# A small load issued earlier, and eight TensorE warm-up matmuls in place of fourteen, at the start of a three-block attention kernel

## The chip, the cores and the metric

The kernel runs on one core of one Trainium2 chip. The metric is device time in microseconds (us) of one execution. The profile adds one profiled execution of the same program. TensorE is called PE in the profile, its weight load PEld, VectorE DVE, ScalarE ACT, GpSimd POOL, and SyncE SP.

## What is computed

Two sequences (b = 0 and 1) of 128 rows by 512 columns go through three residual blocks: a cross-attention block, an RWKV-7 block of which every row is its own short sequence, and an attention block with experts. Only the first block's start is touched by the change:

```python
# x: (2, 128, 512)
h = _layernorm(x, axis=-1)                 # no gain, no bias
Q, K, V = h @ Wq1, h @ Wk1, h @ Wv1
energy = einsum('bqd,bkd->bqk', Q, K)      # causal, masked beyond a counted length
z = softmax(energy / sqrt(32)) @ V
x1 = layer_norm(h + z, ln1_g, ln1_b)
z = cross_attn(x1, ctx_1024, Wq2, Wk2, Wv2)   # 2048 context rows a sequence
...
# RWKV block: x + (xprev - x) * mu_k, mu_a, mu_r, mu_w, mu_v, mu_g, six matmuls
```

The tensor `cols` holds the six mu vectors and the bias of the cross-attention block's first feed-forward layer, turned into 28 columns of 128 numbers.

## The kernel before

Everything is written out by hand, one block of code for each engine, with semaphores between them. An engine works through its list in order, so a wait holds up all that stands behind it. `s_x[b]`, `s_cols` and the `s_place[...]` semaphores count DMA landings; the others (`normed`, `turned`, `prod`, `evict` and so on) count finished steps of an engine, and the index 0 or 1 is the sequence.

**SyncE** issues all loads in one list. `fetch(name)` loads one block of 1 MB (a weight, or 512 context rows) into one of twelve places of `ring`; where the place was used before, it first waits for the block there to be done with. The list begins: X[0], k1, X[1], q1, ct01, `colv`, v1, ct02, ct00, two rows of gains, k2, q2 and on. The reads of `cols` go to `colv` (line 345).

**VectorE** begins with `start(0)`, the statistics of X[0] (lines 858, 860, 862); then, after GpSimd's power for the deviation (line 1786), `norm(0, "x")` (line 866), which gives Y[0]. Then it waits for `s_cols`, computes `rest` = 1 - mu from `colv` (line 1232), and goes on with `start(1)`, `k1_out(0)` (line 905), `norm(1, "x")` (line 866 again), `low("ct01")` (line 888) and `energies(0)`. `rest` itself is first used in the second block, over 100 us later.

**TensorE** begins with 14 matmuls of a matrix of ones into a bank that nobody reads. Then it turns Y[0] with four transposes (`in_halves`, line 416), multiplies by the weights k1 and q1 (`k1(0)`, `q1(0)`, line 442), turns Y[1] (`turned_rows(1, ...)`, line 405), and computes the energies `e1(0)` (line 401, 128x128), the values `v1(0)` (line 401, 128x512), a count, and `k1(1)`. One fp32 matmul stands in the trace as two records (passes). `mm` is the helper of line 401.

**ScalarE** copies the turned halves of Y[0] (`copy_halves`), splits ct01 (`split`, a copy of 128x2048), and evicts the two halves of q1 (`out_halves`), in this order. All its copies have line 1485. `e1(0)` waits for the eviction of q1.

**GpSimd** first makes constants: `ones`, the counters, `ident`, `mhalf`.

Of the kernel before, what the change touches and what calls it, by code (L numbers as in the profile page):

```python
# [76 lines left out]
def build(nc, blocks, xin, vecs, cols, out):  # L77
    with ExitStack() as ctx:
        def sb(name, shape, dt=F32):
            return ctx.enter_context(nc.sbuf_tensor(name, shape, dt))  # L80

        def sem(name):
            return ctx.enter_context(nc.semaphore(name))
# [13 lines left out]
        colv = sb("colv", [128, 28])  # L97
# [133 lines left out]
        s_cols, s_bc0, s_bc1, s_bc2 = (sem(n) for n in ("s_cols", "s_bc0", "s_bc1", "s_bc2"))  # L231
# [80 lines left out]
        def used(name):  # L312

            if name.startswith("ct"):
                return score[int(name[2])].at(name[3])
            if name[0] == "c":
                return gath[int(name[1])].at(name[2])
            return prod[1].at({"rk": "k", "ra": "a", "rw": "w", "rr": "r", "rv": "v", "rg": "g"}.get(name, name))
# [5 lines left out]
        @block_.sync  # L324
        def _(eng):
            s = Waits(eng)

            def fetch(name, first=False):
                before = [m for m in BLOCKS if PLACE[m] == PLACE[name] and NTH[m] == NTH[name] - 1]
                for m in before:  # L330
                    s.wait_ge(*used(m))
                    if m[0] != "c":
                        s.wait_ge(*prod[0].at({"rk": "k"}.get(m, m)))
                eng.dma_start(ring[:, PLACE[name], :], blocks[BLOCKS.index(name), :, :]).then_inc(  # L334
                    s_place[PLACE[name]], 16)

            def spread(first, end):
                return vecs[first:end, :].unsqueeze(0).broadcast_to([128, end - first, 512])

            eng.dma_start(X[0], xin[0, :, :]).then_inc(s_x[0], 16)  # L340
            fetch("k1")
            eng.dma_start(X[1], xin[1, :, :]).then_inc(s_x[1], 16)
            fetch("q1")
            fetch("ct01")
            eng.dma_start(colv[:, :], cols).then_inc(s_cols, 16)
            fetch("v1")
            fetch("ct02")
            fetch("ct00")
            eng.dma_start(bc[:, 0:2, :], spread(0, 2)).then_inc(s_bc0, 16)
            fetch("k2")  # L350
            fetch("q2")
            fetch("ct11")
            eng.dma_start(bc[:, 2:FIRST_BC, :], spread(2, FIRST_BC)).then_inc(s_bc1, 16)
            fetch("ct12")
            fetch("ct10")
            fetch("ct03")
            fetch("c03")
            fetch("ct13")
            fetch("c00")
            fetch("c01")  # L360
            fetch("c02")
            fetch("c10")
            fetch("f1")
            fetch("v2")
            fetch("c13")
            fetch("c11")
            fetch("c12")
            fetch("f2")
            fetch("ro")
            s.wait_ge(*used("c13"))  # L370
            fetch("rw")
            fetch("rk")
            fetch("rv")
            s.wait_ge(*used("c12"))
            fetch("fg")
            fetch("ra")
            s.wait_ge(*used("c11"))
            fetch("rf")
            fetch("fq")
            s.wait_ge(*normed[0].at("n4"))  # L380
            s.wait_ge(*normed[1].at("n4"))
            eng.dma_start(bc[:, 0:len(BCAST) - FIRST_BC, :], spread(FIRST_BC, len(BCAST))).then_inc(s_bc2, 16)
            fetch("rr")
            fetch("fk")
            fetch("fo")
            fetch("rg")
            s.wait_ge(*out_v[0].at("fin"))
            eng.dma_start(out[0, :, :], X[0]).then_inc(s_y[0], 16)
            s.wait_ge(*out_v[1].at("fin"))
            eng.dma_start(out[1, :, :], X[1]).then_inc(s_y[1], 16)  # L390
            s.wait_ge(s_y[0], 16)
            s.wait_ge(s_y[1], 16)
# [4 lines left out]
        def _(eng):  # L397
            s = Waits(eng)

            def mm(o_, l, r, first, last):  # L400
                return t.matmul(o_, l, r, start=first, stop=last)  # L401
# [293 lines left out]
                    i.then_inc(*fo_t[b].inc("fo"))  # L695

            s.wait_ge(*const.at("ones"))
            for _ in range(14):
                mm(psum[:, 7, 0:128], ones[:, :], ones[:, :], True, True)
            s.wait_ge(*const.at("ident"))  # L700
            s.wait_ge(*normed[0].at("x"))
# [1269 lines left out]
```

## Time and profile before

| | us |
|---|---|
| three runs | 237.29, 235.38, 237.14 |
| median | 237.14 |
| profiled execution, its own time | 237.29 |
| its span, first to last instruction | 235.6 |
| PE busy | 226.2 (96%) |
| DVE busy | 162.6 (69%) |
| ACT busy | 92.4 (39%) |
| POOL busy | 77.4 (33%) |

The own time of the profiled execution is 1.7 us over its span; this remainder lies around the first and the last instruction. "Busy" counts an engine's compute instructions, not its waits. Times in a row of the trace are counted from the start of the span. The share `PEclk` is the clock that TensorE was granted: 1.00 is 2.4 GHz, 0.50 is 1.2 GHz. It is a record of changes, so ahead of the first change it shows 1.00 whatever the clock was; there the length of a matmul's record tells it.

### The profile page before, as it was taken

The page shows a single profiled execution, that of the slowest core. Times are in us where ns is not written, and L with a number is a line of the kernel's source. Part 1 is how long each engine was busy: PE and PEld are TensorE (multiplying, and loading weights), DVE is VectorE, ACT ScalarE, POOL GpSimd, SP SyncE. Part 2 cuts the span into 40 slices and gives each one's busy share as a digit, 9 for nine tenths or more (in the row PEclk, how much of TensorE's full clock was granted, in tenths as well). Part 3 has the DMA queues.
Part 4 walks back from the last instruction along what each step waited for, and adds up shares of the span by engine and source line. Part 5 has one row for each costly group of instructions (what it writes and reads, how often), then busy time and mean ns, then how long its engine had stood idle before and what let it go on. Part 6 is the DMA issues. An engine that isn't in the chain of part 4 may idle for free.

```text
span 235.6 us, 3079 instructions
## 1 busy us (share of the span) xinstructions
PE 226.2 (96%) x1148; PEld 160.5 (68%) x1148; DVE 162.6 (69%) x310; ACT 92.4 (39%) x190; POOL 77.4 (33%) x78
## 2 busy tenths in 40 slices
PE   8989999999999999999999999999999699999994
PEld 8976969789888788587384444444444279799951
DVE  2084464696889985970566275699988879798961
ACT  2141415283469668704034244675421201251300
POOL 5040005038426415960051027635223118160000
PEclk9999999999999999999999999999999979999999
DMA  6999899505695599008996499000000000000011
GB/s 242 421 422 395 316 449 388 225 1 179 236 430 224 191 420 426 36 3 314 431 427 252 126 372 424 18 0 0 0 0 4 0 0 0 3 0 1 3 45 45
DMA packets 6351, 43.99 MB, mean 187 GB/s; under 512 B 832, under 2 KB 832, under 8 KB 1472
## 3 DMA queue, kind: packets, MB, share of 16 engines
q1 hardware_dynamic: 6336, 43.80, 46.3%
q8 instruction: 9, 0.15, 0.2%
q14 instruction: 6, 0.05, 0.1%
HBM read 43.27 MB, written 0.52 MB: 186 GB/s over the span
## 4 chain that ended last, share of the span: by engine, by line
PE 86%; DVE 5%; DMA 4%; ACT 2%; SPq 1%; issue 1%; POOL 0%; DVEq 0%
PE psum L401 68%; PE psum L442 13%; DMA colv<-cols 4%; PE psum L405 3%; ACT slots L1485 2%; PE psum L416 1%; DVE small L858 1%; DVE slots L866 1%; PE psum L547 1%; DVE slots L870 1%; SPq L334 1%; POOL small L1786 0%; DVE small L860 0%; DVE psum L1004 0%; DVE slots L882 0%
## 5 line engine op out<-in xcount | busy, mean ns | idle before, releaser
L401 PE MATMUL psum<-ring,slots 128*128 128x512 f32 (+3 forms) x228 | 92.5, 554 | 1.4 <-ACT slots L1485 1.3
L401 PEld LDWEIGHTS psum<-ring,slots 128*128 128x128 f32 (+1 forms) x228 | 40.4, 194 | 42.9 <-issue 37.6
L1485 ACT ACTIVATE slots<-psum 128x256 f32<-128x256 f32 (+4 forms) x58 | 24.4, 447 | 84.7 <-PE psum L401 37.9
L401 PE MATMUL psum<-ring_r,slots_r 128*128 128x512 f32 x192 | 46.2, 396 | 0.0
L1791 POOL TENSOR_TENSOR ring_r<-ring,ring_r 128x640 fp32r<-128x640 f32 x16 | 32.2, 2026 | 30.0 <-ACT ring_r L1485 30.0
L401 PEld LDWEIGHTS psum<-ring_r,slots_r 128*128 128x128 f32 x192 | 35.5, 188 | 9.0 <-ACT slots_r L1485 1.0
L442 PE MATMUL psum<-slots,ring 128*128 128x128 f32 x320 | 37.6, 277 | 0.5 <-ACT slots L1485 0.5
L442 PEld LDWEIGHTS psum<-slots,ring 128*128 128x128 f32 x320 | 36.5, 192 | 1.1 <-ACT slots L1485 1.0
L1485 ACT ACTIVATE ring_r<-ring 128x2048 fp32r<-128x2048 f32 x16 | 30.4, 1913 | 13.0 <-DMA ring<-blocks 7.6
L1786 POOL TENSOR_TENSOR small<-small,mhalf 128x1 f32<-128x1 f32 x16 | 8.8, 552 | 68.7 <-DVE small L862 68.7
L888 DVE TENSOR_TENSOR ring_r<-ring,ring_r 128x1408 fp32r<-128x1408 f32 x16 | 27.5, 1724 | 4.0 <-ACT ring_r L1485 4.0
L1795 POOL TENSOR_TENSOR slots<-slots,bc 128x512 f32<-128x512 f32 x9 | 11.9, 1326 | 15.3 <-DMA bc<-vecs 7.5
L401 PEld LDWEIGHTS psum<-slots,ring 128*128 128x128 f32 x128 | 14.6, 192 | 0.4
L401 PE MATMUL psum<-slots,ring 128*128 128x128 f32 x128 | 14.9, 276 | 0.0
L1485 ACT ACTIVATE slots<-psum,small 128x128 f32<-128x128 f32 (+1 forms) x20 | 8.8, 532 | 6.0 <-PE psum L405 3.3
L416 PEld LDWEIGHTS psum<-ident,slots 128*128 128x128 f32 x44 | 5.0, 141 | 6.9 <-DVE slots L876 2.6
L405 PE MATMUL psum<-ident,slots 128*128 128x128 f32 x60 | 8.3, 276 | 1.3 <-DVE slots L866 1.0
L1485 ACT ACTIVATE slots_r<-psum 128x512 fp32r<-128x512 f32 (+1 forms) x11 | 5.9, 564 | 9.2 <-PE psum L442 5.0
L401 PE MATMUL psum<-slots 64*128 64x128 f32 (+2 forms) x68 | 9.1, 300 | 0.0
L405 PEld LDWEIGHTS psum<-ident,slots 128*128 128x128 f32 x60 | 6.8, 140 | 3.3 <-DVE slots L866 1.2
L1795 POOL TENSOR_TENSOR slots<-slots 128x512 f32<-128x512 f32 x6 | 7.6, 1272 | 3.6 <-ACT slots L1485 2.8
L416 PE MATMUL psum<-ident,slots 128*128 128x128 f32 x44 | 6.9, 279 | 1.9 <-DVE slots L866 1.8
(170 smaller groups left out, 232.8 us busy)
## 6 DMA issues: line engine op xcount, KB each, us to landing
ring<-blocks SPq DMA_DIRECT2D x36, 1024.0 KB, 9.5
bc<-vecs SPq DMA_DIRECT2D x1, 3072.0 KB, 13.3
bc<-vecs SPq DMA_DIRECT2D x1, 1280.0 KB, 6.8
slots<-xin SPq DMA_DIRECT2D x2, 256.0 KB, 3.9
bc<-vecs SPq DMA_DIRECT2D x1, 512.0 KB, 17.4
y<-slots SPq DMA_DIRECT2D x2, 256.0 KB, 2.0
colv<-cols SPq DMA_DIRECT2D x1, 14.0 KB, 9.2
```

The lines of the kernel that those rows point to most:

```text
L334: eng.dma_start(ring[:, PLACE[name], :], blocks[BLOCKS.index(name), :, :]).then_inc(s_place[PLACE[name]], 16)
L401: return t.matmul(o_, l, r, start=first, stop=last)
L405: i = t.transpose(o_[:, c * 128:(c + 1) * 128], x[:, c * 128:(c + 1) * 128], ident[:, :])
L416: i = t.transpose(psum[:, bk1 if c > 1 else bk0, c * 128:(c + 1) * 128], src[:, c * 128:(c + 1) * 128], ident[:, :])
L442: i = t.matmul(psum[:, bk, e * 128:(e + 1) * 128], w[:, c, e * 128:(e + 1) * 128], srcw[:, c, b * 128:(b + 1) * 128], start=c == 0 and (e ...
L547: i = t.matmul(bank(4 * b + n), pick_r[:, n, :], pen_r[b], start=False, stop=True, skip_group_check=True)
L858: v.bn_stats(st[b], x).then_inc(*own_v.inc())
L888: v.tensor_tensor(ring_r[:, p, 0:CUT], ring[:, p, 0:CUT], ring_r[:, high(name), 0:CUT], ALU.subtract).then_inc(*split_low.inc(name))
L1485: return a.activation(o, x, func, **kw)
L1786: g.tensor_tensor(rs[b], ve[b], mhalf[:, 0:1], ALU.pow).then_inc(*rstd[b].inc(name))
L1791: g.tensor_tensor(ring_r[:, p, CUT:], ring[:, p, CUT:], ring_r[:, high(name), CUT:], ALU.subtract).then_inc(*split_lowg.inc(name))
L1795: g.tensor_tensor(o, x, y, op).then_inc(*flag.inc(name))
```

## The change

The load of `colv` moves from the sixth to the second place in SyncE's list, and the loop of matmuls of ones runs 8 times, not 14.

```diff
             eng.dma_start(X[0], xin[0, :, :]).then_inc(s_x[0], 16)
+            eng.dma_start(colv[:, :], cols).then_inc(s_cols, 16)
             fetch("k1")
             eng.dma_start(X[1], xin[1, :, :]).then_inc(s_x[1], 16)
             fetch("q1")
             fetch("ct01")
-            eng.dma_start(colv[:, :], cols).then_inc(s_cols, 16)
             fetch("v1")
...
             s.wait_ge(*const.at("ones"))
-            for _ in range(14):
+            for _ in range(8):
                 mm(psum[:, 7, 0:128], ones[:, :], ones[:, :], True, True)
             s.wait_ge(*const.at("ident"))
             s.wait_ge(*normed[0].at("x"))
```

On SyncE, at the start of the program (`slots<-xin` is X[0], then X[1]; the `ring` rows are, in order, k1, q1, ct01, v1, ct02, ct00):

```order
 L324 UNCONDITIONAL_BRANCH
 L340 DMA slots<-xin 128x512
+L341 DMA colv<-cols 128x28
 L334 DMA ring<-blocks 128x2048
-L342 DMA slots<-xin 128x512
-L334 DMA ring<-blocks 128x2048 x2
-L345 DMA colv<-cols 128x28
-L334 DMA ring<-blocks 128x2048 x3
+L343 DMA slots<-xin 128x512
+L334 DMA ring<-blocks 128x2048 x5
 L349 DMA bc<-vecs 128x1024
```

The load of `colv` has gone ahead of k1, X[1], q1 and ct01; these four now stand one issue later, and everything from v1 on stands where it did.

On TensorE, at the start of the program (the first rows are the matmuls of ones, the transposes of Y[0], and `k1(0)` with `q1(0)`):

```order
 L396 UNCONDITIONAL_BRANCH
-L401 MATMUL psum<-ones 128x128 x14
+L401 MATMUL psum<-ones 128x128 x8
 L416 MATMUL psum<-ident,slots 128x128 x4
 L442 MATMUL psum<-slots,ring 128x128 x32
```

Six matmuls of ones are gone, and nothing else on TensorE moves. The lists of VectorE, ScalarE and GpSimd are the same in both programs.

## Rows read from the trace of the kernel before

**Rows 1.** The page: busy time by engine, share of the span, instructions.
```profile
PE 226.2 (96%) x1148; PEld 160.5 (68%) x1148; DVE 162.6 (69%) x310; ACT 92.4 (39%) x190; POOL 77.4 (33%) x78
```

**Rows 2.** The chain that ended last, its start: start us, us, what.
```profile
3.13 9.20 DMA colv<-cols
12.35 0.18 DVE small L1232
12.53 0.61 DVE small L858
...
14.21 1.92 DVE slots L866
16.13 0.04 issue
16.17 0.66 PE psum L405 x4
```

**Rows 3.** Timeline of PE, 0 to 22 us: start us, us, line, operation, idle before it.
```profile
1.05 6.00 PE L401 MATMUL psum<-ones 128*128 128x128 f32 x28 [1.05 <-POOL ones L1804]
6.89 0.60 PE L416 MATMUL psum<-ident,slots 128*128 128x128 f32 x4
7.75 7.41 PE L442 MATMUL psum<-slots,ring 128*128 128x128 f32 x64 [0.26 <-ACT slots L1485]
16.17 0.66 PE L405 MATMUL psum<-ident,slots 128*128 128x128 f32 x4 [1.01 <-DVE slots L866]
16.66 1.06 PE L401 MATMUL psum<-slots 128*128 128x128 f32 x8
```

**Rows 4.** Timeline of DVE, 0 to 22 us, same columns.
```profile
5.54 0.55 DVE L866 TENSOR_SCALAR slots<-slots,small 128x512 f32<-128x512 f32 x1 [0.74 <-POOL small L1786]
12.35 0.18 DVE L1232 TENSOR_SCALAR small<-colv 128x24 f32<-128x24 f32 x1 [6.27 <-DMA colv<-cols]
13.45 0.68 DVE L905 COPY slots<-psum 128x512 f32<-128x512 f32 x1
```

**Rows 5.** Line 401, records in 1 to 6.2 us and in 6.2 to 7: ns min/median/max, first and last start.
```profile
L401 PE MATMUL psum<-ones x24: 421/421/582, 1.1 to 6.1; 128*128 128x128 f32 x24
...
L401 PE MATMUL psum<-ones x6: 275/336/421, 5.9 to 6.8; 128*128 128x128 f32 x6
```

**Rows 6.** DMA issues of X[0], k1, X[1], q1, ct01, in order: us to landing last.
```profile
slots<-xin SPq DMA_DIRECT2D x1, 256.0 KB, 2.7
...
ring<-blocks SPq DMA_DIRECT2D x1, 1024.0 KB, 5.0
...
slots<-xin SPq DMA_DIRECT2D x1, 256.0 KB, 5.2
...
ring<-blocks SPq DMA_DIRECT2D x1, 1024.0 KB, 7.4
...
ring<-blocks SPq DMA_DIRECT2D x1, 1024.0 KB, 9.5
```

**Rows 7.** Timeline of SP's queue, 0 to 22 us.
```profile
1.22 0.42 SPq L334 DMA_DIRECT2D ring<-blocks  x1
1.70 0.42 SPq L342 DMA_DIRECT2D slots<-xin  x1
2.17 0.92 SPq L334 DMA_DIRECT2D ring<-blocks  x2
3.13 0.44 SPq L345 DMA_DIRECT2D colv<-cols  x1
```

**Rows 8.** Timeline of ACT, 0 to 22 us.
```profile
12.16 1.91 ACT L1485 ACTIVATE ring_r<-ring 128x2048 fp32r<-128x2048 f32 x1 [4.19 <-DMA ring<-blocks]
15.20 0.38 ACT L1485 ACTIVATE slots<-psum 128x256 f32<-128x256 f32 x1 [0.51 <-PE psum L442]
```

**Rows 9.** Windows of PE's line 401: stretch, length, PE, PEld, granted clock, DMA.
```profile
187.48:190.89 3.41, 3.35 (x5) 1.85 (x6) 0.50 0.00 0
190.89:194.30 3.41, 3.41 (x25) 2.90 (x24) 1.00 0.00 0
```

**Rows 10.** Timeline of PE, 180 to 204 us.
```profile
186.62 0.66 PE L416 MATMUL psum<-ident,slots 128*128 128x128 f32 x4 [1.78 <-DVE slots L866]
187.54 4.59 PE L401 MATMUL psum<-ring,slots 128*128 128x400 f32 x8 [0.25 <-ACT slots L1485]
...
199.55 2.85 PE L401 MATMUL psum<-ring,slots 128*128 128x400 f32 x8
```

**Rows 11.** Timeline of DVE, 16 to 118 us: three places behind the start.
```profile
38.96 1.25 DVE L1253 TENSOR_SCALAR bc<-bc 128x512 f32<-128x512 f32 x1 [2.75 <-DMA bc<-vecs]
...
43.00 0.69 DVE L957 TENSOR_TENSOR slots_r<-psum,slots_r 128x512 fp32r<-128x512 f32 x1 [1.87 <-ACT slots_r L1485]
...
47.79 0.75 DVE L876 SCALAR_TENSOR_TENSOR slots<-slots,small,bc 128x512 f32<-128x512 f32 x1
```

**Rows 12.** Timeline of PE, 20 to 110 us: the transposes that wait for the last row above.
```profile
48.60 0.66 PE L416 MATMUL psum<-ident,slots 128*128 128x128 f32 x4
```

## The prediction

> **What bounds the kernel now.** The first view to read is the busy table: TensorE is busy 226.2 of 235.6 us [rows 1]. So a change counts only where it moves TensorE's own work or one of its few waits. The second view is the chain that ended last, read from its start: it does not begin on TensorE but with the load of `colv`, 9.20 us from issue to landing, then VectorE's small operation on line 1232, the statistics of X[1], its norm, and then TensorE's transposes of line 405 [rows 2]. The third is the timeline of TensorE beside that of VectorE. The first real work, the transposes of Y[0], starts at 6.89, right behind the matmuls of ones; k1 and q1 run from 7.75 to 15.16; then TensorE sits idle 1.01 us until VectorE's norm of X[1] is there at 16.13 [rows 2, 3]. VectorE had waited 6.27 us for `colv` [rows 4], for a value that the second block uses. From 16.17 on the chain is nearly all TensorE. So the question is when the transposes of line 405, and `e1(0)` behind them, can start; what they gain or lose there is carried on to the end, unless something late takes its place.
>
> The fourth view is one line's records. The passes of ones take 421 ns each until they start at 6.1, and 275 ns at the end of the loop [rows 5]: TensorE's clock was at its lower level (1.2 GHz) for the first 5.4 us or so of matmuls, and rose to the upper one (2.4 GHz) around 6.5 us. In step from pass to pass this is 0.214 us at the low level (28 passes in 6.00 us, the last few faster) against 7.41 / 64 = 0.116 us for k1 and q1 at the high one [rows 3].
>
> **The load of `colv`.** Removed: VectorE's wait of 6.27 us. `colv` is now issued at 1.22 in k1's place. It lands after 2.7 us at best, the time of X[0] just ahead of it, and after its present 9.20 us at worst: at 1.22 + 2.7 = 3.9 or at 1.22 + 9.20 = 10.4 [rows 2, 6]. Even the worst does: `rest` and the statistics of X[1] take 12.35 to 13.53, some 1.2 us, X[1] itself lands at 1.70 + 5.2 = 6.9 (7.3 with one issue more), so GpSimd has the deviation by 12.3; VectorE then copies k1 (0.68) and does the norm, 0.55 us as in line 866's first row when GpSimd doesn't work beside it and 1.91 when it does [rows 2, 4, 6]. The norm depends on k1(0)'s end, not on `colv`, and is done a good 2 us before q1(0) ends. So the 1.01 us of idle time goes entirely. Added: one issue of 0.44 us in front of k1, X[1], q1 and ct01 [rows 7]. It could delay each landing by between nothing (the transfers are limited by the DMA engines behind it) and 0.44 us; I take 0.44. k1 then lands at 1.22 + 5.0 + 0.44 = 6.7, and `k1(0)` asks for it at 7.1 (below); q1 at 2.17 + 7.4 + 0.44 = 10.0, asked for at 10.8 or later; ct01 at 12.6 instead of 12.16 [rows 6 to 8]. Only the last one is felt: ScalarE splits ct01 until 14.5, and the two evictions of q1 (0.38 each) stand behind it, so that q1 is out at 15.3 at the earliest.
>
> **The six matmuls of ones.** Sixteen passes by 0.214 us end at 1.05 + 3.43 = 4.5. The norm of X[0] ends at 6.09 [rows 4], so the transposes start at 6.13 and not at 6.89: 0.76 us gained, with 1.65 us of idle time on TensorE ahead of them. From the transposes' start to k1's start it was 0.86 us (6.89 to 7.75), ScalarE's copy among it; at the low clock a pass is 0.15 us longer, so k1 starts at about 7.1. Were the clock high from there, q1 would end at 7.1 + 7.41 = 14.5, and the transposes of line 405 would start 16.17 - 14.5 = 1.67 us earlier; with the eviction at 15.3, `e1(0)` starts 16.83 - 15.3 = 1.53 us earlier. That is all the change can win at the start: 0.6% of the time.
>
> **The clock, the cost that decides.** Before, the loop of ones held TensorE busy without a gap until the clock rose, at about 6.5 us. Now the loop ends at 4.5, where the passes still took 421 ns, and TensorE then stands still. So the clock is low when k1 starts. If it stays low for another x us, TensorE does in that time only 0.116 / 0.214 = 0.54 of its work, and loses 0.46 x. The balance at line 405 is 0.46 x - 1.67 us, which is nought at x = 3.6 us. What x is the trace bounds from two rows. Late in the run the clock fell at 187.48 after an idle stretch, and came back at 190.89, after 3.4 us of work [rows 9]; at the program's start it took 5.4 us from the first matmul [rows 5]. Counted from the transposes at 6.13 the shorter gives a rise at 9.5, x = 2.4, balance -0.6 us. Counted from k1's start at 7.1 the longer gives 12.5, x = 5.4, balance +0.8 us. I take 3.4 us counted from k1's start, since the shorter row is also of real matmuls after a pause: x = 3.4, balance -0.1 us. Against the profiled execution's 237.29 this is 237.2; that execution lies 0.15 us over the median of the three, so 237.0.
>
> The Trainium skill, "TensorE: Matmul & The Clock Gate", Part 1, says that the engine is slow by default and activity releases it, and that the point of the rise differs from run to run of the same kernel; the trace shows one rise at the start and agrees that it starts slow, but one trace can't show the spread. Its Part 4 adds that transposes don't count as activity for this; no row separates them here. By that rule the low stretch is counted from k1's start alone, and the balance is -0.1 to +0.8 us by the two rows above. Part 1 also warns that the cost of the rise is under 1% of a usual span, which agrees with the 0.46 x worked out above.
>
> **Rivals.** *The clock costs nothing.* It has risen during the eight matmuls or soon after the transposes, and the 1.65 us of idle time don't hold it back. For it: the rise at 6.5 is one observation, and the idle 1.01 us at 15.16 [rows 3] didn't lower the clock. Against it: no pass was fast before 6.1, and the late fall came behind an idle time of 1.78 us [rows 10], about as long as the new one. Time: 237.14 - 1.53 = 235.6.
>
> *The late fall moves.* `fg(0)`, eight passes of 128x400, took 4.59 us with the clock low and the same for sequence 1 2.85 us with it high [rows 10]: 1.74 us hang on where the fall comes. The lowest of the three runs is 1.76 us under the median, which would fit a run without it. Nothing in the change aims there, but a program whose start has moved could meet it less often. Time: 235.3 with the start balanced, and 233.9 with the start's gain as well, which is the only way to over 1% faster that I see. It could as well be met in more runs, but the median already has it.
>
> *The gain is won and lost behind.* The norm of x1 of sequence 1 ends at 48.54 and TensorE takes it at 48.60 [rows 11, 12], 0.06 us of room. But the chain to it starts from k2's copy, at 43.00 after 1.87 us of waiting for ScalarE and so for TensorE, and would move along; the load of the gains, which VectorE gets at 38.96 after waiting [rows 11], has those 1.87 us of room even if it doesn't move at all. So 1.53 us can pass. Were it all lost the time would be 237.1, in the main case's range.
>
> *Slower.* The clock misses its rise at k1 and stays low through k1 and q1, as the first matmuls after a pause look the same to it as the ones did at 1.05 to 6.1. All 64 passes at 0.214 take 13.7 us and not 7.41: 6.3 us lost, less 1.67, is +4.6 us, 241.7. It is over 1% slower from x = (2.37 + 1.67) / 0.46 = 8.8 us on. Against it: in both rows the clock rose within 5.4 us of work.
>
> *The change doesn't do what it says.* `colv` would have to land after 12 us from the second place of the list, or k1 be held up by it by over a microsecond; X[1], issued third, landed at 6.9 [rows 6, 7], so I give this almost nothing, and the first would only leave the time as it is.
>
> **How the numbers follow.** A measurement of this kernel can tell about 1%, 2.4 us, from no change. Balanced start, the gain lost behind and the last rival among it: 0.60, 236.5 to 238.0, likeliest 237.0. The clock costs nothing: 0.23, 235.6. The late fall moved or missed in most runs: 0.10, 235.3, and of it 0.03 with the gain, 233.9. Slower, a long low stretch: 0.07, 238 to 241.7, of which 0.05 is over 1%. The range from 235.1 to 238.4 leaves out 233.9 and the greater part of the slow case. Faster by over 1% has 0.05 (233.9, and a little for an underrated gain), slower 0.05, the rest 0.90.
>
> **What would show it.** In the changed kernel's profile: the load of `colv` gone from the chain, and no wait of VectorE on line 1232; eight matmuls of ones, all passes near 421 ns, ending at 4.5; transposes of line 416 at 6.13; k1's passes first at 421 ns and then at 275 ns, with the step between them at 9.5 to 12.5 us; no idle time ahead of line 405, which starts at 15.6 to 17.0. If k1's passes are at 275 ns from the first one on, the first rival holds, and line 405 starts near 14.5. The prediction is wrong if line 405 starts outside this stretch, or if it starts early and the end doesn't follow.

## The result, and the profile after

The change made the kernel slightly slower: 237.75 us against 235.53, medians of 20 runs each, a ratio of 1.0086 with a 95% interval of 1.0064 to 1.0108. Here and below the ratio is not the quotient of the two medians (that would be 1.0094): where the runs lie in two groups a median jumps from one to the other, so the ratio with its interval is what a verdict rests on. It leaves out the few runs that are more than 1.5% slower than the fastest of their kernel. Two things about the runs have to be seen with the result. The median of before, 237.14 over three runs, had been a small sample: 15 of its 20 runs lie at 235.3 to 235.9 and five at 237.1 to 237.3. And the runs of the changed kernel are not in two tight groups but spread from 236.25 to 239.27.

The chain of the changed kernel, from its start (start us, us, what), answers to [rows 2]:

```profile
1.70 6.38 DMA ring<-blocks
8.08 0.14 issue
8.22 10.19 PE psum L442 x64
18.41 0.44 PE psum L405 x4
18.85 0.13 issue
18.98 1.13 PE psum L401 x8
```

`colv` is gone from the chain, but k1 has taken its place: it is issued at 1.70 and lands at 8.08, where before it was issued at 1.22 and landed at 6.2 [rows 6]. Behind it the same 64 passes take 10.19 us and not 7.41 [rows 3]. TensorE's timeline shows the same, and what is ahead of it:

```profile
1.05 3.78 PE L401 MATMUL psum<-ones 128*128 128x128 f32 x16 [1.05 <-POOL ones L1804]
6.23 1.08 PE L416 MATMUL psum<-ident,slots 128*128 128x128 f32 x4 [1.40 <-DVE slots L866]
8.22 10.19 PE L442 MATMUL psum<-slots,ring 128*128 128x128 f32 x64 [0.90 <-DMA ring<-blocks]
18.25 0.60 PE L405 MATMUL psum<-ident,slots 128*128 128x128 f32 x4
```

The transposes of line 416 start at 6.23, 0.1 us behind the forecast, but take 1.08 us where they took 0.60. Line 405 has no idle time ahead of it any more, and starts at 18.25: 2.08 us later than the 16.17 of before. The records of line 442, in the stretches 8 to 13.6 us and 13.9 to 18.4 us (ns min/median/max, first and last start), show the clock:

```profile
L442 PE MATMUL psum<-slots,ring x25: 421/421/553, 8.2 to 13.5; 128*128 128x128 f32 x25
...
L442 PE MATMUL psum<-slots,ring x39: 275/275/421, 13.7 to 18.1; 128*128 128x128 f32 x39
```

The first 26 of the 64 passes, up to the one that starts at 13.7, are slow ones. The clock rose at about 14 us, six microseconds after k1 began, and 7.5 us later than before [rows 5]. It had risen neither in the loop of ones nor ahead of the transposes, whose passes take 418 ns. The ones:

```profile
L401 PE MATMUL psum<-ones x16: 421/421/582, 1.1 to 4.4; 128*128 128x128 f32 x16
```

VectorE waits no more for `colv`; line 1232 runs right behind the norm, and the norm of X[1] takes 0.54 us where it took 1.92 beside GpSimd [rows 2]:

```profile
6.00 0.17 DVE L1232 TENSOR_SCALAR small<-colv 128x24 f32<-128x24 f32 x1
8.76 0.69 DVE L858 BATCH_NORM_STATS2 small<-slots 128x6 f32<-128x512 f32 x1 [2.59 <-DMA slots<-xin]
...
15.48 0.54 DVE L866 TENSOR_SCALAR slots<-slots,small 128x512 f32<-128x512 f32 x1
```

The transfers tell in part why k1 is late. These are the windows 2:3, 3:4 and 4:5 of the changed kernel; the last two columns are the DMA engines' busy share and GB/s:

```profile
2.00:3.00 1.00, 1.00 (x7) 1.00 (x6) 0.00 (x0) 0.08 (x1) 1.00 (x3) 1.00 0.82 242
3.00:4.00 1.00, 1.00 (x7) 1.00 (x7) 0.30 (x1) 0.00 (x0) 0.51 (x4) 1.00 0.91 185
4.00:5.00 1.00, 0.83 (x4) 0.54 (x3) 0.73 (x3) 0.00 (x0) 0.05 (x1) 1.00 0.87 360
```

and the same three of the kernel before:

```profile
2.00:3.00 1.00, 1.00 (x7) 1.00 (x6) 0.00 (x0) 0.08 (x1) 1.00 (x3) 1.00 0.95 295
3.00:4.00 1.00, 1.00 (x7) 1.00 (x7) 0.30 (x1) 0.00 (x0) 0.51 (x4) 1.00 0.89 356
4.00:5.00 1.00, 1.00 (x6) 1.00 (x6) 0.73 (x3) 0.00 (x0) 0.05 (x1) 1.00 0.99 410
```

The engines are busy for nearly as long (2.60 us of the 3, against 2.83), but move 0.79 MB in these 3 us where they moved 1.06. That is 0.27 MB, some 0.7 us at the 410 GB/s that they reach afterwards; with the later issue (0.48 us) it makes 1.2 of the 1.9 us by which k1 is late. The rest is not explained here; k1's landing also differs between traces with the same order of loads, as below.

### The profile page after: what moved, and what is told of

Its sections match the earlier page's. It is cut to its first block, busy times and chain, and to the rows that moved or that the text cites. A ratio compares the mean times of both kernels' runs of the same rounds, so it can differ in the third digit from the quotient of the medians.

```text
span 236.3 us, 3055 instructions
## 1 busy us (share of the span) xinstructions
PE 225.8 (96%) x1136; PEld 160.5 (68%) x1136; DVE 163.6 (69%) x310; ACT 92.6 (39%) x190; POOL 79.0 (33%) x78
## 4 chain that ended last, share of the span: by engine, by line
PE 89%; DVE 4%; DMA 3%; ACT 2%; issue 1%; SPq 0%; POOL 0%; DVEq 0%
PE psum L401 67%; PE psum L442 17%; PE psum L405 3%; DMA ring<-blocks 3%; ACT slots L1485 2%; PE psum L416 1%; PE psum L547 1%; DVE small L858 1%; DVE slots L870 1%; DVE psum L1004 0%; DVE slots L876 0%; DVE slots L882 0%; DVE psum L1114 0%; DVE slots L1226 0%; DVE small L860 0%
## 5 line engine op out<-in xcount | busy, mean ns | idle before, releaser
L401 PE MATMUL psum<-ring,slots 128*128 128x512 f32 (+3 forms) x228 | 90.8, 546 | 1.4 <-ACT slots L1485 1.3
L401 PEld LDWEIGHTS psum<-ring,slots 128*128 128x128 f32 (+1 forms) x228 | 39.6, 190 | 42.1 <-issue 36.0
L1791 POOL TENSOR_TENSOR ring_r<-ring,ring_r 128x640 fp32r<-128x640 f32 x16 | 32.7, 2059 | 35.0 <-ACT ring_r L1485 35.0
L442 PE MATMUL psum<-slots,ring 128*128 128x128 f32 x320 | 40.4, 289 | 1.2 <-DMA ring<-blocks 0.9
L442 PEld LDWEIGHTS psum<-slots,ring 128*128 128x128 f32 x320 | 39.3, 204 | 1.9 <-ACT slots L1485 1.8
L888 DVE TENSOR_TENSOR ring_r<-ring,ring_r 128x1408 fp32r<-128x1408 f32 x16 | 28.7, 1801 | 4.0 <-ACT ring_r L1485 4.0
L1795 POOL TENSOR_TENSOR slots<-slots,bc 128x512 f32<-128x512 f32 x9 | 11.9, 1327 | 15.3 <-DMA bc<-vecs 7.5
L401 PEld LDWEIGHTS psum<-slots,ring 128*128 128x128 f32 x128 | 14.6, 192 | 0.4
L401 PE MATMUL psum<-slots,ring 128*128 128x128 f32 x128 | 14.9, 276 | 0.0
L416 PEld LDWEIGHTS psum<-ident,slots 128*128 128x128 f32 x44 | 5.3, 147 | 8.6 <-DVE slots L876 2.6
L858 DVE BATCH_NORM_STATS2 small<-slots 128x6 f32<-128x512 f32 x6 | 4.2, 694 | 6.4 <-POOL mhalf L1817 3.7
```

The lines of the kernel that those rows point to most:

```text
L416: i = t.transpose(psum[:, bk1 if c > 1 else bk0, c * 128:(c + 1) * 128], src[:, c * 128:(c + 1) * 128], ident[:, :])
L442: i = t.matmul(psum[:, bk, e * 128:(e + 1) * 128], w[:, c, e * 128:(e + 1) * 128], srcw[:, c, b * 128:(b + 1) * 128], start=c == 0 and (e ...
L858: v.bn_stats(st[b], x).then_inc(*own_v.inc())
L888: v.tensor_tensor(ring_r[:, p, 0:CUT], ring[:, p, 0:CUT], ring_r[:, high(name), 0:CUT], ALU.subtract).then_inc(*split_low.inc(name))
L1791: g.tensor_tensor(ring_r[:, p, CUT:], ring[:, p, CUT:], ring_r[:, high(name), CUT:], ALU.subtract).then_inc(*split_lowg.inc(name))
L1795: g.tensor_tensor(o, x, y, op).then_inc(*flag.inc(name))
```

## The experiments

All edits are against the kernel before unless it says otherwise. "Landing" is k1's, and the start of `e1(0)` is that of line 401's 128x128 passes behind the transposes of line 405. Beside a median stands that of 35 runs of before on the same chip; E1 to E4, E5 to E8 and E9 to E12 were on three chips, so that their medians compare best through the ratio to before.

**E1, the early load alone; E2, the shorter loop alone.** E1 is the change with `range(14)` kept; E2:

```diff
-            for _ in range(14):
+            for _ in range(8):
```

> The load of colv in second place, the loop of ones still 14 long. Theory A (the loss is the clock: with 8 ones it is low through most of k1 and q1, and this costs 2.8 us; the early load costs some 1.9 us in k1's landing, half of it hidden): k1 still lands at about 8.1 and starts at 8.2, but its passes are at 275 ns from the first on, q1 ends near 15.6 and line 405 starts near 15.7, 0.5 us ahead of 16.17; time 235.0 against 235.5 before. Theory B (the loss is the early small load alone, through the DMA engines): the time is near the change's 237.7, and line 405 starts near 18.

> Eight ones, the load of colv in its old place. Theory A: k1 lands at 6.2 again and starts at 7.1 with the clock low; it rises some 5 to 6 us later, q1 ends at 16.5 to 17.5, line 405 starts there with no idle time ahead; time 236.0 to 237.0. Theory B: the clock is of no matter, line 405 stays at 16.17 behind the late colv, and the time is 235.5.

E1: 235.84 against 235.69, ratio 1.0013 (0.9977 to 1.0048). E2: 235.81, ratio 1.0004 (0.9966 to 1.0041). Neither part alone costs what both cost together. TensorE's start in E1, whose own time was 234.78:

```profile
1.05 5.28 PE L401 MATMUL psum<-ones 128*128 128x128 f32 x28 [1.05 <-POOL ones L1804]
6.22 0.63 PE L416 MATMUL psum<-ident,slots 128*128 128x128 f32 x4
7.36 7.38 PE L442 MATMUL psum<-slots,ring 128*128 128x128 f32 x64 [0.51 <-ACT slots L1485]
14.58 0.60 PE L405 MATMUL psum<-ident,slots 128*128 128x128 f32 x4
15.64 1.13 PE L401 MATMUL psum<-slots 128*128 128x128 f32 x8 [0.46 <-ACT slots L1485]
```

With 14 ones the clock was high for all of k1 and q1 in this execution, so theory A's point holds; k1 landed at 7.2 here, earlier than expected, and the start was better than expected for it. `e1(0)` waited for the eviction of q1, as the prediction had it. But 235.84 is over the 235.0 of the expectation: five of the twelve runs lie at 236.7 to 238.2. E2 (own time 235.80) shows a third course of the clock, in the windows of 1 us from 7 to 12 (the third number from the end is the granted clock):

```profile
7.00:8.00 1.00, 0.89 (x7) 0.89 (x8) 0.00 (x0) 0.33 (x2) 0.00 (x0) 0.90 0.97 410
8.00:9.00 1.00, 1.00 (x6) 1.00 (x6) 0.00 (x0) 0.00 (x0) 0.00 (x0) 0.50 0.99 418
...
10.00:11.00 1.00, 1.00 (x7) 1.00 (x6) 0.00 (x0) 0.00 (x0) 0.00 (x0) 0.50 1.08 459
11.00:12.00 1.00, 1.00 (x10) 1.00 (x10) 0.00 (x0) 0.13 (x1) 0.00 (x0) 0.90 1.02 383
```

It had risen at the end of the ones, fell at 7.8 after the idle time, with k1 already running, and was back at 11.2. k1 and q1 took 9.04 us, 1.6 more than at the high clock. The late norm was done at 15.83, and line 405 started behind q1 without idle time at 15.99, no later than in before: the wait for `colv` hid this loss.

**E3, the wait removed without touching the loads; E4, the same with 8 ones.**

```diff
             norm(0, "x", Y[0], X[0])
-            s.wait_ge(s_cols, 16)
-            v.tensor_scalar(rest, colv[:, 0:24], ...)
             start(1)
...
             weigh(0)
+            s.wait_ge(s_cols, 16)
+            v.tensor_scalar(rest, colv[:, 0:24], ...)
             k1_out(1)
```

> Fourteen ones and colv in its old place, but VectorE computes rest (and waits for colv) behind weigh(0), at about 24 us, where colv has long landed. This takes VectorE's wait away without touching the loads. Theory A: k1 starts at 7.75 with the clock high, q1 ends at 15.16, line 405 starts at 15.2, 1.0 us earlier than before; time 234.5. Rival (the time won is lost again behind, as at the norm of x1 of sequence 1): line 405 at 15.2 but the time stays at 235.5.

> As e3, with eight ones. Theory A: TensorE's start is that of e2, since q1 ends after colv's norm there anyhow; line 405 at 16.5 to 17.5, time 236.0 to 237.0, some 2 us over e3. Theory B (the clock is of no matter): k1 at 7.1, line 405 at 14.6, time 233.9.

E3: 235.94 against 235.69, ratio 0.9983 (0.9954 to 1.0011), spread from 234.17 to 237.78. In its trace line 405 started at 15.08, as expected, but `e1(0)` then waited 0.36 us for ScalarE and started at 16.04, 0.6 us earlier than before and not 1.0; its own time of 235.06 shows that this was not lost behind. E4: 237.35, ratio 1.0013 (0.9975 to 1.0050), from 235.06 to 239.64. The medians lie 1.4 us apart, on the side on which the change and E1 do, but the intervals of the two ratios overlap, so this pair alone would not show that 8 ones cost something. And E4's profiled execution started best of all:

```profile
1.05 3.78 PE L401 MATMUL psum<-ones 128*128 128x128 f32 x16 [1.05 <-POOL ones L1804]
6.22 0.63 PE L416 MATMUL psum<-ident,slots 128*128 128x128 f32 x4 [1.39 <-DVE slots L866]
7.11 7.41 PE L442 MATMUL psum<-slots,ring 128*128 128x128 f32 x64 [0.25 <-ACT slots L1485]
14.36 0.60 PE L405 MATMUL psum<-ident,slots 128*128 128x128 f32 x4
15.08 1.13 PE L401 MATMUL psum<-slots 128*128 128x128 f32 x8
```

None of its 16 passes of ones was fast (421 ns, the last one from 4.4 us on), but the transposes were (273 ns, where the change has 418): the clock rose between 4.8 and 6.2 us, while TensorE stood idle, and stayed up through k1 and q1. Up to the transposes TensorE's rows are the same as the change's. So with 8 ones the clock's course is not the same in every execution. And in E3 k1 landed at 7.7, with all loads in their old order: its landing varies of itself as well.

**E5 and E6, 20 ones: with the early load, and with E3's edit.**

> The change with 20 ones in place of 8. Theory A (the loop of ones is what makes the clock high at k1 in every execution; with 14 it mostly was, with 8 it is left to chance): no execution starts k1 low, the loop ends at 6.5 to 7.5, k1 starts when it lands, 7.3 to 8.1, line 405 at 14.8 to 15.7; times 234.7 to 235.3, or 1.8 us more where the clock falls late; the median under e1's 235.84 or equal to it. Theory B (the early colv is the loss, not the clock): as the change, 237 or more.

> e3 with 20 ones: the wait of VectorE gone, the loads in their old order. Theory A: the clock is high at k1 always; line 405 at 15.0 to 15.8, set by the loop's end or by k1's landing; times 234.2 to 235.1, or 1.8 us more with the late fall; the median 0.5 to 1 us under before. Rival (the chance is in k1's landing and not in the clock): the same spread as e3, 234.2 to 236.5.

E5: 236.04 against 237.07, ratio 0.9982 (0.9953 to 1.0010). E6: 235.78, ratio 0.9985 (0.9951 to 1.0020). In the trace of neither is the clock low beyond the loop, but the loop itself was longer than forecast where the clock rose late: in E5 it lasted 7.62 us, and k1 started at 9.36. Theory A's mechanism holds, its sizes were too good, and B is out: with the early load and 20 ones no run passed 237.34, and the ratio's interval ends below the change's. E6's rival, that the chance is in k1's landing, is not excluded: its nine runs with a mean clock of 0.999 or 1.0 spread from 234.82 to 236.35, no less than E3's four with such a clock. A part of that is the loop itself, which ended at 7.4 in E6's trace and at 8.7 in E5's.

**E7, the small load twice**, with 14 ones:

```diff
             eng.dma_start(colv[:, :], cols).then_inc(s_cols, 16)
+            eng.dma_start(TMP[1][:, 0:28], cols).then_inc(s_cols, 16)
```

> As e1 (14 ones, colv in second place), with the same 14 KB loaded a second time right behind it, into a place that is free then. If the 128 small packets cost the stream of loads at the front: the DMA engines move still less at 2 to 5 us than in e1 (209 and 319 GB/s at 3 to 5 us), k1 lands 0.7 to 1.2 us later than in e1, at 8.0 to 9.2, and the median is 0.7 to 1.2 us over e1's. If k1's late landing in the change was chance (in e3 it landed at 7.7 with colv in its old place): the issue's 0.4 us alone.

235.39 against 237.07, ratio 0.9958 (0.9927 to 0.9989); it looks faster because before met a fall of the clock in 21 of its 35 runs on this chip (E8, below), and E7 in 4 of 10. k1 was issued at 2.2 and landed at 7.8, 0.6 us later than in E1 but earlier than in the change, which has the load once. The runs without a late fall (below) have a median of 235.09, as E1's with 235.10. The DMA engines did move less, 109 and 272 GB/s at 3 to 5 us where E1 has 209 and 319, but the forecast of 0.7 to 1.2 us for a second load fell: most of the 0.6 us is the one issue more. So I can't put the whole lateness of k1 in the change down to the small packets.

**E8, ones in the late gap**, the kernel before otherwise:

```diff
             rf(1)
+            for _ in range(7):
+                mm(psum[:, 7, 0:128], ones[:, :], ones[:, :], True, True)
             s.wait_ge(*normed[0].at("n5"))
```

> The kernel before, with 7 matmuls of ones between rf(1) and the transposes of the last norm of sequence 0, where TensorE waits 1.8 us for VectorE. If the group of runs of before at 237.0 to 237.4 is the one in which the clock falls in this gap: the group is gone, all runs lie at 235.3 to 235.8 and none has a mean clock under 0.998. If not, the two groups stay.

235.49 against 237.07, ratio 0.9956 (0.9929 to 0.9983). 11 of 12 runs lie at 235.36 to 235.67; of before's 35 runs beside it 21 lay at 236.92 to 237.94, all of them with a mean granted clock of 0.990 to 0.993, and the other 14 at 235.33 to 235.91. Before's two groups are thus, nearly all of it, the clock's fall in this one gap, or its absence; one run of E8 at 237.14, with a mean clock of 0.990, shows that a fall of the same price is still met with the ones there. The gap in E8:

```profile
185.00:187.00 2.00, 1.78 (x16) 1.55 (x15) 1.30 (x4) 0.40 (x1) 0.55 (x1) 1.00 0.00 0
187.00:189.00 2.00, 1.75 (x7) 0.97 (x6) 1.78 (x5) 0.66 (x2) 0.55 (x1) 1.00 0.00 0
```

where before the clock fell to 0.50 at 187.48 [rows 9].

On the other two chips 5 of before's 70 runs lie at 238.7 to 238.8 with a mean clock of 0.983, the price of two falls; where the second one is no trace shows.

The traces also give a rule for reading all of them. Own time less the start of `e1(0)`, in us:

| kernel | start of e1(0) | own time | difference |
|---|---|---|---|
| E1 | 15.64 | 234.78 | 219.14 |
| E3 | 16.04 | 235.06 | 219.02 |
| E6 | 16.10 | 235.20 | 219.10 |
| E8 | 16.55 | 235.59 | 219.04 |
| E2 | 16.71 | 235.80 | 219.09 |
| E5 | 17.33 | 236.45 | 219.12 |
| the change | 18.98 | 238.05 | 219.07 |
| before, with the late fall | 16.66 | 237.29 | 220.63 |
| E4, with the late fall | 15.08 | 235.84 | 220.76 |
| E7, with the late fall | 15.99 | 236.68 | 220.69 |

What TensorE gains or loses ahead of `e1(0)` is carried to the end, to within 0.13 us from trace to trace, and a late fall adds 1.6 us. The four traces that follow keep to it: E9 219.10, E10 219.05, and with the late fall E11 220.72 and E12 220.74. So by its start the change stood 2.3 us behind before, and only its lack of a late fall made the two profiled executions look close.

**E9, the best of the parts:** E3's edit (14 ones, loads in their old order) and E8's.

> 14 ones, VectorE's wait for colv moved behind weigh(0), loads in their old order, and the 7 ones in the late gap. In all traces so far without a late fall the own time was the start of e1(0) plus 219.0 to 219.1 us, and with one about 220.7. If both parts add up: e1(0) at 15.1 to 16.1, no late fall, times 234.2 to 235.2 in nearly all runs, median 234.9, ahead of before's better group (235.3 to 235.7) and 2.2 us ahead of its other one. Rival (the ones in the late gap only move the fall elsewhere once the start has moved): a group at 236 to 237 stays.

234.60 against 235.58, ratio 0.9946 (0.9915 to 0.9976). Nine of twelve runs lie at 234.19 to 235.03, three at 235.69 to 235.76. Its profiled execution had `e1(0)` at 15.85 and 234.95. It is faster than before by 0.5%, clear of noise, and so faster than the change as well. How much of it is the moved `rest` is not separated: E8 alone, on another chip, had 0.9956, and its main group lies 1.1 us above E9's.

**E10, the change with the 7 late ones.**

> The change with the 7 ones in the late gap, so that its runs differ by their start alone. If the loss of the change lies at the start: median 237.2 to 237.8, spread from 235 to 238, e1(0) at 16 to 19 us, none of the runs as tight as before's. If it lies in more late falls than before's: the median drops to 235.5 to 236.

236.91 against 235.58, with runs from 234.61 to 239.12; the interval of the ratio, 0.9960 to 1.0046, holds 1. The spread stays without the late gap in play: the five runs with a mean clock of 0.998 or more, in which no fall was recorded, lie between 234.61 and 237.82. So it is at the start. The median is 0.3 us under what I expected and 0.8 under the change, so a part of the change's loss may be late falls: 8 of its 21 executions have a mean clock of 0.985 or 0.986, twice the loss of one late fall. E10 has three such runs itself (238.45 to 239.12), so not every second fall is the one in the late gap. Nor are late falls all of the difference: among the runs without a recorded fall the change's eight have a median of 237.6 and E10's five one of 235.97, with the same start. The two were on different occasions, and why the poor starts were commoner in the change's runs is not shown. The profiled execution of E10 had k1 landing at 8.1 and then a low stretch of 3.4 us:

```profile
6.23 0.63 PE L416 MATMUL psum<-ident,slots 128*128 128x128 f32 x4 [1.39 <-DVE slots L868]
8.21 9.01 PE L442 MATMUL psum<-slots,ring 128*128 128x128 f32 x64 [1.36 <-DMA ring<-blocks]
17.06 0.60 PE L405 MATMUL psum<-ident,slots 128*128 128x128 f32 x4
```

Its program is the change's up to the late gap, and TensorE's rows up to the transposes agree with the change's to 0.01 us. Yet its transposes ran at the high clock, 272 ns against 418: here too the clock had risen in the idle time behind the ones, and in the change it had not.

**E11, `colv` behind k1 and not ahead of it,** 8 ones:

```diff
             eng.dma_start(X[0], xin[0, :, :]).then_inc(s_x[0], 16)
-            eng.dma_start(colv[:, :], cols).then_inc(s_cols, 16)
             fetch("k1")
+            eng.dma_start(colv[:, :], cols).then_inc(s_cols, 16)
```

(against the change).

> The change with colv issued right behind k1 instead of ahead of it; 8 ones. If it is the 128 small packets ahead of k1 that hold k1 up: k1 lands at 6.1 again and starts at 7.1, colv lands at 5 to 7 and is in nobody's way, the times are those of e4 (235.1 to 238, median 237.3) or a little better, 0.4 to 1 us under the change. If the late landing of k1 is chance: as the change, 237.7.

235.87 against 235.58, ratio 1.0002 (0.9969 to 1.0036), 1.9 us under the change's median, though the two weren't timed side by side. k1 landed at 6.4 and started at 7.11, `colv` landed at 6.6:

```profile
1.05 3.44 PE L401 MATMUL psum<-ones 128*128 128x128 f32 x16 [1.05 <-POOL ones L1804]
...
7.11 9.04 PE L442 MATMUL psum<-slots,ring 128*128 128x128 f32 x64 [0.25 <-ACT slots L1485]
15.99 0.60 PE L405 MATMUL psum<-ident,slots 128*128 128x128 f32 x4
```

In this trace, beside the change's, the swap of two neighbours in SyncE's list takes 1.1 us off k1's start, as forecast; the median lies further below the change's than the 0.4 to 1 us of the forecast. That the shorter idle time ahead of k1 (0.25 us where the change had 0.90) also helped the clock is possible, but not shown: in this trace the clock fell at 7.4 all the same.

**E12, the change with 11 ones.**

> The change with 11 ones, between its 8 (237.75) and e1's 14 (235.84). The loop would end at 5.8 with the clock low, against the transposes at 6.2. If the idle stretch ahead of the transposes is what lets the clock be low at k1: nearly as good as e1, median 236.0 to 236.5. If only the number of matmuls done by then matters: in the middle, near 236.8.

236.20 against 235.58, ratio 0.9976 (0.9939 to 1.0014). With the early load, 8, 11, 14 and 20 ones give ratios to before of 1.0086, 0.9976, 1.0013 and 0.9982 (medians of 237.75, 236.20, 235.84 and 236.04); the intervals of the last three overlap, and each ends below the first's. The gain comes with the first three, with which the loop lasts until about 6 us and meets the transposes; that speaks for the idle stretch, as the first case had it. In its trace k1 landed as late as in the change, and yet ran at the high clock:

```profile
1.05 5.06 PE L401 MATMUL psum<-ones 128*128 128x128 f32 x22 [1.05 <-POOL ones L1804]
6.23 0.63 PE L416 MATMUL psum<-ident,slots 128*128 128x128 f32 x4
8.07 7.38 PE L442 MATMUL psum<-slots,ring 128*128 128x128 f32 x64 [1.22 <-DMA ring<-blocks]
15.29 0.60 PE L405 MATMUL psum<-ident,slots 128*128 128x128 f32 x4
```

This trace beside the change's is the clock's price at its plainest: the same landing, 8.07 and 8.22 as the start, and 2.8 us between the starts of `e1(0)` (16.21 and 18.98).

## Why the prediction was wrong

**What bounds the start** was right: VectorE's wait was removed, the idle 1.01 us ahead of line 405 went, and what happens ahead of `e1(0)` reaches the end in full, which the table shows for ten executions. That nothing is lost behind it was right too. One reading was off: the most that `e1(0)` could gain was counted from 16.83, but it had started at 16.66 [rows 3], so that 15.3 is 1.36 us earlier and not 1.53. This is not what failed.

**The load of `colv`** is the first term that was mis-sized. The prediction added the issue, 0.44 us, to k1's landing and took the transfer itself for nothing, and concluded: "Only the last one is felt", which is ct01. k1 landed at 8.08 instead of 6.7; the transposes were done at 7.3, and TensorE then stood idle 0.90 us, where 0.26 had gone to ScalarE's copy before. In the traces with `colv` ahead of k1 and loaded once, k1 landed at 7.2 to 8.1; with `colv` behind it at 6.1 to 6.4, but for E3's 7.7. The bound at 0.44 us should have been open upwards. That the load itself has a part in it shows in what the DMA engines moved from 3 to 4 us: 108 to 209 GB/s in the six traces with `colv` ahead of k1, 287 to 408 in the eight others.

**The clock** is the term in which it failed: "I take 3.4 us counted from k1's start", x = 3.4, from the late episode's row. In the profiled execution k1 began 1.1 us later and the clock was low for another 5.9 us, beyond even the prediction's upper 5.4, and the 64 passes lost 2.78 us, where the prediction had 1.57. The price of 0.46 us for each of these microseconds held (0.46 x 5.9 is 2.7); the number of them failed. By its own signs the prediction is wrong too: the step between slow and fast passes came at 14 us, not at 9.5 to 12.5, and line 405 started at 18.25, not at 15.6 to 17.0. The loss, 1.2% of the span, is also over the 1% that the prediction took for the usual bound. Against the forecast end of q1 (7.1 + 7.41 + 1.57 = 16.1) 1.1 us are k1's later start and 1.2 the clock: 18.4, where 18.41 was measured. The step was wrong in kind and not only in size: one row of one episode was taken as the value of something that differs between executions. The runs show at least three courses with 8 ones: risen ahead of the transposes and kept (E4, loss nothing), risen by then, fallen at 7.4 to 8.4 and back 3.4 us later (E2, E10 and E11, loss 1.6), and not risen until 14 (the change, loss 2.8). The first rival, "the clock costs nothing", is true of E4's execution; the slower rival, x of 8.8 us and more, was seen in none.

The Trainium skill, "TensorE: Matmul & The Clock Gate", Part 1, says that the point of the rise differs from run to run of the same kernel. The traces agree: after the same rows of TensorE the clock was up by 6.2 us in E4 and E10 and rose at 14 in the change. So the outcome should have been written as a spread, and the times have one, from 236.25 to 239.27 in the change. Before had no such spread at its start, because the late `colv` held line 405 at about 16.1 whatever the clock and k1 did. That cover is what the prediction overlooked: it counted the removed wait as pure gain, and it had been hiding up to 1.6 us of lateness of either kind, from 14.5 us, where q1 ends at best, to 16.1. E2's trace shows it for the clock.

**The late fall** was seen as a rival and sized at 1.74 us; it measured 1.6. But the prediction called it what "the median already has". 15 of 20 runs of before don't have it, so the baseline was 1.6 us too high, and the sum, made against the profiled execution of 237.29, which had the fall, inherited this. The forecast time of 237.0 is near the measured 237.75 only because a baseline too high and a loss left out nearly cancel: against 235.53 the same working gives 235.4, and the time is 2.3 us over it. That the measured time lies in the stated range is therefore luck.

**What stays open.** Why k1 lands at 7.2 in one trace and at 8.1 in another with the same order of loads: the moved bytes at 2 to 5 us explain 0.7 us, E7 shows that a second small load doesn't add as much, and E3 shows a late landing without any. What decides whether the clock rises behind 8 ones or stays low is open as well, and so is how often each course comes: E10, with the change's start, has a ratio of 1.0003 where the change has 1.0086, and the intervals do not overlap. And how the 21 executions of the change divide among the courses of the clock can't be read from their mean clock alone, since what lies ahead of the first recorded rise doesn't count in it. With the time beside it, it tells a part: eight of them have a mean clock of 0.998 or more, so no fall was recorded, and seven of the eight lie at 236.88 to 238.05. By the table's 219.1 their `e1(0)` started at 17.8 to 19.0 (an estimate), where E12, with k1 about as late and the clock high, had 16.21. So the late first rise of the profiled execution is probably no rarity, though only one trace shows it. E4's group at 237.3 to 237.7 fits a slow start with a late fall, but no trace shows that.

## What to carry to other kernels

A wait that is about to be removed may be hiding other work's variation: ask what the cases beneath it look like at their worst, not only in the one trace. Matmuls that bring the clock up are worth their time as long as they reach, nearly without a gap, to the first real work, and a single gap late in a run can deserve some as well. If a small load is early only because somebody asks for it early, move the asking: E3's edit takes the wait away as the early load does, without putting anything ahead of the load that is really needed. Neither is a gain clear of noise by itself; with the matmuls in the late gap, E9, E3's edit is part of one.

## What the runs showed of the hardware that I had not expected

- With a load of 14 KB in 128 rows of 112 bytes issued ahead of k1, the DMA engines moved 185 GB/s at 3 to 4 us where they had moved 356, at the same busy share (0.91 and 0.89); the five other traces with it there have 108 to 209, and E11, with it behind k1, has 311.
- With 8 ones all passes of ones were slow (421 ns, the last from 4.4 us on), and in E4 and E10 the transposes at 6.2 us were fast (272 ns): the clock rose while TensorE stood idle. In the change, with the same rows up to there, it did not.
- In E2, E10 and E11 the granted clock fell at 7.8, 8.4 and 7.4 us, with k1 already running. The idle stretches ahead of it (1.55, 1.39 and 1.74 us behind the ones, and 0.26, 1.36 and 0.25 us ahead of k1) were over by then: the fall comes after the work is back. E4 had 1.39 and 0.25 us there and no fall.
- Two groups of runs 1.6 us apart, which one would take for noise of the measurement, were for the most part one gap in which the clock falls or doesn't; seven matmuls there whose result nobody reads left one group (11 of 12 runs within 0.3 us).
